# A transformer-layer kernel: products of ones at the start, beta by pairs behind the token loop, and embedding gathers four tiles ahead

## The reference, cut to what matters

```
tok = wte[input_ids]                               # 2 x 1024 rows of 192 numbers
Q = layer_norm(tok, gamma, beta) @ W_proj.T        # 8 heads of 64
V = tok @ W_val.T
mask = tokens 1..S-2 that are in link_ids;  denom = max(mask.sum() * 8, 1)
Q_store = Q[:, :-2] * mask;   Q_erase = Q_store / norm(Q_store)
traces = 0.99 * (vt - Q_erase^T Q_erase vt / denom) + 0.1 * Q_store^T V[2:] / denom
h = (Q shifted by one token) @ traces @ W_out.T
h = h + attention(layernorm(h));   h = h + experts(layernorm(h))
```

## Time and profile before

| | |
|---|---|
| median of 3 runs | 464.32 us |
| the profiled execution | 464.32 us, span 462.5 us |
| TensorE busy | 431.2 us, 93% of the span |
| VectorE busy | 297.3 us, 64% |
| ScalarE busy | 228.5 us, 49% |
| GpSimd busy | 145.4 us, 31% |
| the token front and the setup behind it | about the first 85 us |

### The profile page before, as it was taken

How to read it: one execution, slowest core, us unless ns; L and a number is a source line. 1 busy time by engine, 2 the same in 40 slices (tenths; PEclk the granted TensorE clock), 3 DMA queues, 4 the chain that set the end, 5 groups by cost and what they waited for, 6 DMA issues and landing times.

```text
span 462.5 us, 8303 instructions
## 1 busy us (share of the span) xinstructions
PE 431.2 (93%) x3086; PEld 356.7 (77%) x3086; DVE 297.3 (64%) x776; ACT 228.5 (49%) x415; POOL 145.4 (31%) x235
## 2 busy tenths in 40 slices
PE   5889998999888999999999989999999889999995
PEld 2667755798777888988888878899975577787895
DVE  6489873586765577676777676766965243443564
ACT  4577742588743446554232566877874312122220
POOL 5778600375010065120003490003540331212310
PEclk9999999999999999999999999999999999999999
DMA  3343000200100000500000000003629999999404
GB/s 97 111 126 104 11 2 0 103 1 1 30 0 0 1 0 1 206 1 0 1 0 1 1 1 0 2 0 132 280 100 412 388 351 380 382 373 386 152 19 136
DMA packets 14231, 49.64 MB, mean 107 GB/s; under 512 B 3504, under 2 KB 8528, under 8 KB 9968
## 3 DMA queue, kind: packets, MB, share of 16 engines
q1 hardware_dynamic: 7584, 43.21, 24.8%
q0 software_dynamic: 2912, 3.37, 2.6%
q10 hardware_dynamic: 3696, 2.54, 1.8%
HBM read 45.94 MB, written 3.15 MB: 106 GB/s over the span
## 4 chain that ended last, share of the span: by engine, by line
PE 69%; DMA 12%; DVE 11%; POOL 3%; issue 2%; ACT 2%; SPq 0%; POOLq 0%; ACTq 0%; DVEq 0%
DMA w1r<-in_p_w 10%; PE ps L907 9%; PE ps L953 8%; PE ps L1110 6%; PE ps L1051 3%; PE ps L889 3%; PE ps L1080 2%; PE ps L933 2%; DMA tok<-in_L_tok_wte,ints 2%; PE ps L937 2%; PE ps L936 2%; PE ps L934 2%; PE ps L935 2%; PE ps L1097 2%; PE ps L854 1%
## 5 line engine op out<-in xcount | busy, mean ns | idle before, releaser
L907 PE MATMUL ps<-pr,et 128*128 128x192 f32 x256 | 46.6, 333 | 2.1 <-DVE et L1768 1.6
L1110 PE MATMUL ps<-ys,ct 128*128 128x192 f32 x256 | 45.2, 331 | 1.7 <-DMA ys<-ys_dram 1.7
L1937 DVE TENSOR_TENSOR res<-ps,res 128x384 f32<-128x384 f32 x64 | 35.7, 558 | 15.2 <-PE ps L1110 10.7
L907 PEld LDWEIGHTS ps<-pr,et 128*128 128x128 f32 x256 | 41.1, 189 | 5.4 <-ACT et L1332 3.1
L1110 PEld LDWEIGHTS ps<-ys,ct 128*128 128x128 f32 x256 | 41.2, 190 | 5.1 <-issue 4.8
L501 POOL TENSOR_SCALAR ve<-mv 128x1 f32<-128x1 f32 x32 | 12.1, 378 | 94.8 <-DVE mv L1783 54.0
L585 POOL DMA_DIRECT2D ys<-ys_dram x32 | 19.6, 617 | 69.8 <-DMA ys_dram<-ysb 68.7
L1451 ACT ACTIVATE hs<-ps 128x384 f32<-128x384 f32 x16 | 7.8, 490 | 58.5 <-PE ps L1051 58.5
L1321 ACT ACTIVATE scs<-ps,pr 128x1024 f32<-128x1024 f32 x16 | 17.8, 1115 | 29.2 <-PE ps L858 29.2
L1325 ACT ACTIVATE zz<-zz,nmx 128x1024 f32<-128x1024 f32 x16 | 18.4, 1150 | 27.7 <-DVE nmx L1762 27.4
L1928 DVE COPY ysb<-ps 128x192 f32<-128x192 f32 x16 | 5.7, 356 | 39.0 <-PE ps L1080 39.0
(11 more groups left out here) (318 smaller groups left out, 1197.6 us busy)
## 6 DMA issues: line engine op xcount, KB each, us to landing
w1r<-in_p_w SPq DMA_DIRECT2D x16, 1152.0 KB, 19.4
w2r<-in_p_w SPq DMA_DIRECT2D x16, 1152.0 KB, 19.2
ys_dram<-ysb ACTq DMA_DIRECT2D x16, 96.0 KB, 8.3
ys<-ys_dram POOLq DMA_DIRECT2D x32, 48.0 KB, 7.2
phT<-in_p_phi SPq DMA_DIRECT2D x1, 1024.0 KB, 4.6
wT<-in_p_qkv SPq DMA_DIRECT2D x1, 774.0 KB, 4.2
out<-res SPq DMA_DIRECT2D x3, 192.0 KB, 3.3
out<-res ACTq DMA_DIRECT2D x3, 192.0 KB, 3.8
```

The source lines that it names most:

```text
L907: last = mm(d[:, 0:D], et[:, k, :], pr[:, b * KT + k, 1:1 + D], start=(k == 0), stop=(k == KT - 1))
L1110: last = mm(bank(5 + q % 3)[:, h * D:(h + 1) * D], ct[:, u % 2, k + h, :], ys[:, t % YR, b, :], start=True, stop=True)
L1937: v.tensor_tensor(res[:, i:i + 2, :], bank(5 + q % 3)[:, 0:2 * D].rearrange("p (h d) -> p h d", h=2), res[:, i:i + 2, :], ALU.add).then_in ...
```

## The change: what it does

Six edits, all in the front and the setup:

- TensorE multiplies a 128 x 128 tile of ones by itself nine times before it waits for its first inputs.
- W_proj times beta is no longer made by eight products ahead of the loop and kept in `bpair`, but by four products ahead of kB2, from the row of beta; VectorE copies it out of PSUM.
- The row of beta is one row, not two: VectorE drops the second copy of it behind `beta`, kB2, nB2 and vB2. The count of masked tokens is read in VectorE's step 2 and waited for at the q product of tile 2.
- The factors of tiles 0, 1 and 2 are made one by one, between the first gathers.
- GpSimd's step i issues gather i + 4, not i + 6.
- `ahead` is {2: [3, 4], 3: [5], 4: [6], 5: [7], 6: [8, 9]}, then s + 3. TensorE's `cprime` comes one step later.

```
-            front_factors(1, 3)
+            front_factors(1, 2)
+            gather(3)
+            front_factors(2, 3)
+            gather(4)
             pool.wait_ge(m["mask_ready"], 1)
             masked(0)
-            gather(5)
-            gather(6)
             for i in range(1, NT):
-                if i + 6 < NX:
-                    gather(i + 6)
+                if i + 4 < NX:
+                    gather(i + 4)
                 masked(i)
                 if i % 2 and i + 2 < NT:
                     front_factors(i + 2, min(i + 4, NT))
...
+            pe.wait_ge(m["ones_ready"], 1)
+            for k in range(9):
+                mm(bank(2)[:, 0:P], ones[:], ones[:], start=True, stop=True)
             pe.wait_ge(m["in_tok"], 16 * 2)
             pe.wait_ge(m["in_wp"], 16)
...
-            for t in range(HP):
-                c, o = slice(t * P, (t + 1) * P), slice(2 + 2 * t, 4 + 2 * t)
-                mm(bank(3)[:, o], wpT[:, 0, c], betA, start=True, stop=False)
-                last = mm(bank(3)[:, o], wpT[0:DB, 1, c], betB, start=False, stop=True)
...
-                if 2 <= s < NT + 2:
-                    cprime(s - 2)
+                if 3 <= s < NT + 2:
+                    cprime(s - 3)
+                if s == NT + 1:
+                    cprime(NT - 1)
...
             pe.wait_ge(m["setup_taken"], at["kA"] + 1)
+            for t in range(HP):
+                mm(setup_bank("kB2")[:, 272 + 2 * t:274 + 2 * t], wpT[DB:DB + 1, 1, t * P:(t + 1) * P],
+                   ones[DB:DB + 1, 0:2], start=True, stop=True)
             prepare("kB2", at["kA"] + 1)
...
-                    link(remainder(B2[DB:DB + 2, :], d[DB:DB + 2, 0:n], scale[2], B2[DB:DB + 2, :]))
-                    last = v.tensor_scalar(B2[DB:DB + 1, :], d[DB:DB + 1, 0:n], scale[3], None, ALU.mult)
+                    last = remainder(B2[DB:DB + 1, :], d[DB:DB + 1, 0:n], scale[2], B2[DB:DB + 1, :])
...
-                if s <= 4:
-                    return {2: [3, 4], 3: [5], 4: [6, 7]}.get(s, [])
+                if s <= 6:
+                    return {2: [3, 4], 3: [5], 4: [6], 5: [7], 6: [8, 9]}.get(s, [])
                 return [s + 3] if s + 3 < NT else []
```

More of the change, by code:

```diff
@@ L184, in build @@
         eyeP = sb("eyeP", [P, DT], where=front)
-        bpair = sb("bpair", [P, 2 * HP], where=front)
         r1 = sb("r1", [P, HP, DT], where=front)
@@ L640, in _ @@
             pe.wait_ge(m["mask_ready"], 1)
-            pe.wait_ge(m["ones_ready"], 1)
-            mm(bank(3)[:, 0:1], ones[:], msum[:], start=True, stop=True)
-            for t in range(HP):
-                c, o = slice(t * P, (t + 1) * P), slice(2 + 2 * t, 4 + 2 * t)
-                mm(bank(3)[:, o], wpT[:, 0, c], betA, start=True, stop=False)
-                last = mm(bank(3)[:, o], wpT[0:DB, 1, c], betB, start=False, stop=True)
-            last.then_inc(m["cnt_filled"], 1)
+            mm(bank(6)[:, 0:1], ones[:], msum[:], start=True, stop=True).then_inc(m["cnt_filled"], 1)
             def slots(b, s):
@@ L680, in q_proj @@
                     pe.wait_ge(m["beta_ready"], 1)
-                if i == 1:
+                if i == 2:
                     pe.wait_ge(m["cnt_ready"], 1)
@@ L1516, in round_off @@
                 else:
-                    link(remainder(B2[DB:DB + 2, :], d[DB:DB + 2, 0:n], scale[2], B2[DB:DB + 2, :]))
-                    last = v.tensor_scalar(B2[DB:DB + 1, :], d[DB:DB + 1, 0:n], scale[3], None, ALU.mult)
+                    last = remainder(B2[DB:DB + 1, :], d[DB:DB + 1, 0:n], scale[2], B2[DB:DB + 1, :])
                 if name == "kB2":
-                    last = v.tensor_copy(wpn[:, :, XC:PC], bpair[:].rearrange("p (t c) -> p t c", c=2))
+                    last = v.tensor_copy(wpn[:, :, XC:PC], d[:, 272:272 + 2 * HP].rearrange("p (t c) -> p t c", c=2))
                 last.then_inc(m["setup_taken"], 1)
             def round_k(name):
-                round_off(name, [SCALE] * 4, *(t[:, 0:XC + 1] for t in kv), XC + 1)
+                round_off(name, [SCALE] * 3, *(t[:, 0:XC + 1] for t in kv), XC + 1)
             def round_v(name):
-                round_off(name, [1.0] * 4, *(t[:, XC + 1:KV] for t in kv), D + G)
+                round_off(name, [1.0] * 3, *(t[:, XC + 1:KV] for t in kv), D + G)
             def round_n(name):
-                round_off(name, (gamA, gamB[DB:P], gamR[DB:DB + 2], gamR[DB:DB + 1]), nAh[:], nAl[:], nB1[:], nB2[:], D)
+                round_off(name, (gamA, gamB[DB:P], gamR[DB:DB + 1]), nAh[:], nAl[:], nB1[:], nB2[:], D)
             def stats(i):
@@ L1541, in _, with count @@
             remainder(wpAl[:], wpT[:, 0, :], gamA, wpAh[:])
+            stats(1)
             dve.wait_ge(m["wp_hi"], 2)
-            link(remainder(wpB1[DB:P, :], wpT[DB:P, 1, :], gamB[DB:P], wpB1[DB:P, :]))
-            stats(1)
+            remainder(wpB1[DB:P, :], wpT[DB:P, 1, :], gamB[DB:P], wpB1[DB:P, :])
+            stats(2)
             dve.wait_ge(m["setup_hi"], 1)
[L1546 to L1555, removed]
+            beta_row = setup_bank("beta")[DB:DB + 1, :]
+            v.tensor_tensor(wpB2[DB:DB + 1, :], beta_row, f(wpB2[DB:DB + 1, :]), ALU.subtract).then_inc(m["beta_ready"], 1)
+            def count():
+                dve.wait_ge(m["cnt_filled"], 1)
+                link(v.tensor_scalar(cnt[:, 0:1], bank(6)[:, 0:1], float(HEADS), 1.0, ALU.mult, ALU.max))
+                link(v.reciprocal(cnt[:, 1:2], cnt[:, 0:1]))
+                v.tensor_scalar(cnt[:, 2:3], cnt[:, 1:2], -TRACE_DECAY * ERASE_LR, None, ALU.mult)
+                v.tensor_scalar(cnt[:, 3:4], cnt[:, 1:2], TRACE_LR, None, ALU.mult).then_inc(m["cnt_ready"], 1)
             def lo_parts(i):
@@ L1591, in ahead @@
             def ahead(s):
-                if s <= 4:
-                    return {2: [3, 4], 3: [5], 4: [6, 7]}.get(s, [])
+                if s <= 6:
+                    return {2: [3, 4], 3: [5], 4: [6], 5: [7], 6: [8, 9]}.get(s, [])
                 return [s + 3] if s + 3 < NT else []
             dve.wait_ge(m["xl_ones"], 1)
-            dve.wait_ge(m["cnt_ready"], 1)
             for s in range(NT + 4):
@@ L1603, in _ @@
                     dve.wait_ge(m["cprime_done"], NT)
+                    dve.wait_ge(m["cnt_ready"], 1)
                     v.tensor_scalar(cc[:, 0, :], bank(5)[:, 0:D], gamA, cnt[:, 3:4], ALU.mult, ALU.mult)
@@ L1611, in _ @@
                     stats(i)
+                if s == 2:
+                    count()
                 if s == KT + 2:
@@ L1614, in _ @@
                 if s == NT + 1:
-                    v.tensor_copy(wpT[DB:DB + 1, 1, :], beta_row[0:1]).then_inc(m["setup_taken"], 1)
+                    v.tensor_copy(wpT[DB:DB + 1, 1, :], beta_row).then_inc(m["setup_taken"], 1)
                     for r in range(2):
```

## The result

The changed kernel takes 478.15 us (median of four runs, 477.72 to 484.56). The kernel before, beside it, took 464.35. The ratio is 1.031, with a 95% interval of 1.026 to 1.035: 3.1% slower, and inside the forecast range. The profiled execution took 477.72 us around a span of 475.9, against 464.32 and 462.5 before. So 13.4 us have to be found.

A forecast was written before the change was run, and what follows sets the result against it. Bound: TensorE and VectorE both full, on a ring of VectorE, GpSimd and DMA. 464.3 + 11.7 (loop: 4.9 by tile 5 including the head's gain, plus 6.8) + 0.3 (tail) = 476.3, rounded to 476.0; range 470.5 to 481.

The forecast's parts named there:

- The mechanism: Front loop: VectorE's statistics, GpSimd's factors and next gather, and its DMA landing form a ring; VectorE waits for each turn.
- Head: Head of the loop: fewer gathers stand ahead of the factors, so tile 3's xh starts 2.3 us sooner (bounds 1.5, 3.3).
- Gather 9: Statistics of tile 8 on VectorE: their gather lands late beside the wvT and vt loads; wait 2.8 us, 0.7 without collision.
- First ring: VectorE, statistics of tile 9: they wait for statistics 8 to go once round the ring (4.47 us); stall 4.41 us.
- Pair stalls: VectorE, statistics of tiles 11, 13 and 15: the same ring less one step's work, 2.27 us each, together 6.8.
- The rival by which only the first ring bites: Later loop: VectorE finds slack, so the three pair stalls are covered; 469.2 us, chance 0.10.
- The clock in the loop: TensorE in the loop: 0 in the sum; a rival had idling drop it to 1.2 GHz, chance 0.05.
- the rival's first case: Loop after the first long gap: TensorE at 1.2 GHz for two steps only, mostly swallowed by the next stall; +0 to 2.9.
- The renewed fall at each stall: Loop, same clock rival: each stall throttles TensorE again, a pair takes 11.6 us instead of 8.05; chance 0.05 for the rival.
- the rival's 486.8: Total time in us if each stall renews TensorE's 1.2 GHz, three pairs adding 10.6; chance 0.05 for the rival.
- Ones: TensorE's start: the nine products of ones stay off the path, 0 us (ends +1.0 and -0.9).
- Tail: Setup behind the loop: four products before kB2 cost 1.1 us, dropped copies give back; sum +0.3, ends -0.5 and +1.5.

The follow-up runs named there:

- experiment 1: Changed kernel with gathers issued six ahead again (i + 6, gathers 5 and 6 ahead of the loop): 466.34 us, ratio 1.0008 to the kernel before.
- experiment 2: Kernel before with one edit, GpSimd issuing gather i + 4 and none ahead of the loop: 476.42 us, ratio 1.0236.
- experiment 3: Changed kernel with gathers 10, 12, 14 and 16 each one place forward, ahead of the pair's factors: 467.09 us, ratio 1.0043 to the kernel before.
- experiment 5: Changed kernel without the nine products of ones: 477.73 us, ratio 1.0293 to the kernel before.
- experiment 6: Kernel before plus the nine products of ones alone: 465.30 us, ratio 1.0008.
- experiment 7: Kernel before with four products ahead of kB2 replacing the eight ahead of the loop, beta still two rows: 466.99 us, ratio 1.0052.
- experiment 9: Kernel before with the four products behind kB2 in a bank of their own, replacing the eight ahead of the loop: 465.37 us, ratio 1.0003.
- experiment 10: Kernel before with the four products ahead of kB2, plus six filler products of ones behind kB2: 466.67 us, ratio 1.0012.
- experiment 4: Changed kernel with TensorE's waits filled by 26, 8, 8 and 8 products of ones ahead of q products 5, 7, 9, 11: 476.33 us, ratio 1.0242.
- experiment 8: Changed kernel with gathers 5 to 10 spread over steps 1 to 4, then six ahead: 467.22 us, ratio 1.0030 to the kernel before.
- experiment 11: Experiment 8 with the four products behind kB2: 466.38 us, ratio 1.0014 to the kernel before.
- experiment 12: Experiment 11 plus twelve products of ones ahead of tile 5's q product and six behind kB2: 467.39 us, ratio 1.0045 to the kernel before.

## Why the prediction was right, and what in it was not

The forecast was 476.0 with a range of 470.5 to 481; measured 478.15. The mechanism was the one named, shown by experiments 1 to 3.

*Head.* The xh of tile 3 starts at 16.88 (17.3 forecast, 19.54 before) and that of tile 5 at 23.99 (23.8). Right.

*Gather 9.* Issued at 26.51 (26.3 forecast), landed in 3.79. The forecast took 4.8 for the collision with the loads of wvT and vt. So statistics 8 wait 1.69 and not 2.8. The size lay between the two ends that were given (0.7 and 2.8); in experiment 5 it was 2.92.

*First ring.* 4.43, forecast 4.41. The chain gives its pieces: 1.68 from `ve` (31.09) over rstd and nmr to the issue of gather 10 (32.77), 2.79 for the landing. The Trainium skill (DMA: Bandwidth & Descriptors, "Anatomy of one DMA — SWDGE (gpsimd) path") would have 2.2 for such a landing; the trace does not agree here either: the smallest of all 18 is 2.6. The XL of tile 5 starts at 36.32, 4.27 later than before (4.9 forecast; what is missing is gather 9).

*Pair stalls.* 2.26, 2.23 and 2.21, in sum 6.70; 6.8 forecast. From 47.85 on the q products come in steps of 5.50, 2.88 and 5.18 (2.9 and 5.2 forecast). The rival by which only the first ring bites is refuted.

*The clock in the loop.* Here the sum was short. 4.27 and 6.70 make 10.97, but the product with `cc` is 12.64 late. Of the missing 1.67, 1.55 is the step from tile 11 to tile 12: 4.41 instead of 2.86, in the stretch with a clock of 0.69. The forecast took 0 for it and priced a dip at up to 2.9 only at the range's end. After the first gap of 7.17 us the clock was low as well (0.50), but the next pair stall swallowed that, as the rival's first case had it. The Trainium skill (TensorE: Matmul & The Clock Gate, "HAM oscillation — how this bites in real kernels") expects a fall after such a long idle gap, and the trace agrees. The later two falls stand beside gaps of 2.25 and 1.16 us. The renewed fall at each stall did not come in this execution: 53.35 and 56.23 are one full-speed step apart, 2.88. In experiment 5 it did come (q products at 54.48 and 59.67 take 0.80), and the next stall swallowed most of it. So the rival's 486.8 (476.3 and 10.6 make 486.9) was not reached even there.

*Ones.* 0 forecast, 0 measured (experiments 5 and 6).

*Tail: the term that was mis-sized.* Forecast +0.3, of it 1.1 for the four products. These cost 0.97 where they stand (kB2's turn starts at 89.86 instead of 77.22, which is the 12.64 of the loop, and its other products 0.97 behind that); the turn itself is 0.45 shorter, since VectorE drops a copy. So +0.52, which is where the 13.16 come from. But the 24 products behind lasted 1.37 longer, since the clock fell from 90 to 95 us (0.76). So the setup lost 1.89 where the forecast had "ends -0.5 and +1.5". The step that failed is that the sum knows the products' own time and the copies, and puts the clock behind them at nothing. Experiments 7, 9 and 10 show that in the kernel before, otherwise unchanged, the fall comes with the products ahead of kB2 and goes with their place or with a filled gap. In the changed kernel the cause stays open: the same products stand ahead of kB2 in experiments 1, 3, 4 and 5, after the same gap of 1.16, and the 24 products take 4.09.

*Behind the setup* 1.13 came back, where the forecast counted nothing. In the profiles, from the start of the mixing to the end of the span it is 376.3 in the changed kernel, 376.1, 376.7, 376.6 and 376.4 in experiments 4, 1, 5 and 8, in which VectorE also drops the second copies of the row, and 377.4, 377.7, 377.7 and 377.3 in the kernel before and experiments 9, 7 and 6, in which it makes them. Experiments 3 and 11 drop them too and took 377.8 and 377.4, with a clock dip between 140 and 150 us. That fits the dropped copies; no experiment took them alone.

Together: 4.27 + 6.70 + 1.67 for the loop, 0.52 + 1.37 for the setup, 1.13 back: 13.4. The clock is 2.9 of it (1.55 and 1.37), in experiment 4, at full clock in these places, the mixing starts 2.8 sooner, and without them the time is 474.8. So the forecast's 476.0 was near the truth partly by luck, since errors met: 0.6 too much at gather 9 and no gain behind the setup, against 2.9 too little for the clock.

What stays open is how often each dip comes over the executions. The profiled one was the shortest of the four (477.72, mean clock 0.977); the longest (484.56) was at 0.955. Open in part is why experiment 8 gains nothing: its loop still has the wait of 2.0 us for the gather beside wvT and TensorE's gap of 2.9 behind it, and in experiment 11, the same loop, `cc` comes at 65.96, against 64.31 before. Experiment 12 shows only that keeping the clock there doesn't bring `cc` sooner.

## What to carry to other kernels

When a prefetch is moved in an in-order queue, don't ask how many tiles it is ahead; ask which instruction stands right in front of it, what that waits for, and whether the consumer comes next on its engine. If all three close into a ring, each turn costs the whole ring less the work between two turns, and cutting the ring at one place (experiment 3) gives back nearly all. Small products ahead of a serial turn cost their own time, and in experiment 7 a fall of the clock on what follows as well; the same products one place later, in the engine's gap, are free (experiment 9). Price a possible clock fall into the range, but don't take one profile's fall for a property of the edit: look whether kernels with the same edit have it too.

## What the runs showed of the hardware

- The granted clock falls without a long gap too. In experiment 7 the longest idle time next to the fall (80 to 85 us) is 1.61 us, and four small products stand ahead of it. In the kernel before and in experiments 6 and 9, without products at that place, the same stretch is granted 1.00. But the products are neither needed nor enough: experiment 2 has the fall without them (5.77 for the 24 products, idle 1.62 before), and of seven profiles with them after an idle time of 1.16 or 1.61 us, three have it (the changed kernel 5.46, experiments 7 and 8 5.77) and four don't (experiments 1, 3, 4 and 5, 4.09 each). Cost: 1.4 to 1.7 us.
- Dips come in places that no edit touches. Experiments 3, 10 and 11 kept the clock in the setup and had a dip between 140 and 150 us, where before has 1.00. The stretch from 140 to 145 us, first before, then experiment 10:

```profile
140.00:145.00 5.00, 3.82 (x26) 3.68 (x27) 3.29 (x9) 1.22 (x2) 0.00 (x0) 1.00 0.00 0
```

```profile
140.00:145.00 5.00, 2.99 (x17) 2.67 (x16) 3.98 (x8) 0.59 (x1) 0.00 (x0) 0.84 0.00 0
```

  Whether a shift in the setup brings such a dip is not shown, since executions of one kernel differ as well: the kernel before, beside experiments 9 to 12, took from 463.23 us (mean clock 0.999) to 468.82 (0.989). Differences under 0.3% need many executions here.
- The clock that the profile shows for the first microseconds is not to be trusted: the kernel before is granted 1.00 there in every slice, but its products take 0.88 instead of 0.51, and the changed kernel shows 0.57 from 10 to 15 us for the same kind of product. The duration of a product of known size is the better clock.
- A gather of 96 KB beside the 512 KB load of wvT took 3.79 us to land in the changed kernel, 4.76 in the kernel before, 5.03, 5.49 and 5.88 in experiments 5, 8 and 12. The gather of 17.33 in the changed kernel, beside the load of wT, took 4.62; its others took 2.6 to 2.8.
